# Moving the layer norm's scaling of the 16-row attentions from VectorE to ScalarE

## The chip, the cores and the metric

One core of one Trainium2 chip runs the whole program as a single launch. The metric is device time in microseconds (us). The kernel before took 4759.7 us (median of 3 runs, 4759.58 to 4760.19).

Engine names in the rows: PE is TensorE (PEld its weight loads), DVE is VectorE, ACT is ScalarE, POOL is GpSimd, SPq is SyncE's DMA queue.

## What is computed

The reference is a residual stack of four layers on x of shape 8 x 512 x 256, each an attention and a feed-forward part behind a layer norm. The part that matters here is its first three steps, which share one form: norm, 16 heads of width 16, softmax over 512 keys, output projection, residual.

```python
def _layernorm(x, axis=-1, eps=1e-05):
    m = jnp.mean(x, axis=axis, keepdims=True)
    v = jnp.var(x, axis=axis, keepdims=True)
    return (x - m) / jnp.sqrt(v + eps)
...
x = x + _L0_xattn_ref(_layernorm(x, axis=-1), ctx_1024, ctx_1024, ...)
x = x + _L0_ffn_ref(_layernorm(x, axis=-1), ...)
x = x + _L1_xattn_ref(_layernorm(x, axis=-1), ctx_1024, ...)
```

The second of the three is an attention of x on itself, whose output is scaled by gates (the "mixture").

## The kernel before

The function `softmax_attentions` runs these three steps as 24 **items**: 3 layers x 8 sequences of 512 rows. Items 0 to 7 and 16 to 23 are of kind "cross" (keys and values from the context), items 8 to 15 of kind "mixture". In the trace they fill the stretch from 0 to about 1800 us.

**Rounds and steps.** Every engine has its own instruction stream, and all of them walk the same loop: one round for each item q, 32 steps n in a round. In each step PE makes two score tiles (L715, into `ps_sc`), two tiles from which the maxima are taken (L726, into `ps_max`) and, at odd steps, eight matmuls of probabilities by values (L737). ACT makes one exponential of 1024 columns per step (L642, `probs`). DVE takes two row maxima per step (L461, `maxes`), twelve steps ahead of the exponentials. Both `ps_max` and `ps_sc` are double-buffered.

**The one bank that is shared.** Everything else (transposes, projections, the norm of a later item) goes through a single PSUM bank, `ps_t`. The table `TURNS` says at which step PE fills it with what, and which engine empties it; PE's stream waits until the previous content is taken. The entries of the steps that matter are, for a cross item, 11 and 12 "hT" (the previous item's heads, copied out by ACT, L672), 13 "negmax" (negated maxima of a group of heads, PE L789, copied out by ACT in 1.86 us, L655), 14 "xnT" (the transposed norm of the item two rounds ahead, PE L744, ACT L672), 15 "raw". For a mixture item it is 4 "raw", 5 "negmax", 7 and 8 "xnT".

**The norm.** It is made for the item two rounds ahead (`ahead`). `NORM_AT` sets its start: step 6 where that item is a cross one, step 0 where it is a mixture. From the start on: two steps of `bn_stats` on DVE, then `moments` on DVE (`mv`, L433), then `rstd_of` on POOL (`vareps` L337, `rstd` L340). Four steps after the start and five steps after it, DVE runs `normalised`, two tiles of 128 x 256 each time (L439, `xn`), at the end of the step. When all four tiles of `xn` are done, POOL's `bias` adds the output bias to the item's rows of x (L347, cross items alone), and PE may transpose `xn`.

**Negated maxima.** `negated` (DVE L468 and L470) closes a group of heads; in a cross round group 2 is closed at step 11, between the two calls of `normalised`.

**Splits.** POOL's `split` (L356 to L363) makes the bf16 parts of queries and keys in four operations of about 2 us.

Of the kernel before, what the change touches and what calls it, by code (L numbers as in the profile page):

```python
# [16 lines left out]
F32 = mybir.dt.float32  # L17
BF16 = mybir.dt.bfloat16
U32 = mybir.dt.uint32
ALU = mybir.AluOpType  # L20
ACT = mybir.ActivationFunctionType
AX = mybir.AxisListType

P = 128
# [3 lines left out]
TILES = S // P  # L28
# [102 lines left out]
NORM_AT = {"cross": 6, "mixture": 0}  # L131
# [13 lines left out]
def softmax_attentions(nc, T, G, name, kind):  # L145
# [13 lines left out]
    with Phase(nc, name) as ph:  # L159
# [9 lines left out]
        mv = ph.sb("mv", [P, TILES, 2], F32)  # L169
        vareps = ph.sb("vareps", [P, TILES], F32)  # L170
        rstd = ph.sb("rstd", [P, TILES], F32)
        xn = ph.sb("xn", [P, TILES, D], F32)
        xnT = ph.sb("xnT", [P, C, S], F32)
        qf = ph.sb("qf", [P, C, S], F32)
# [53 lines left out]
        score_ps, probs_ready, probs_used, out_taken = (ph.sem("score_ps"), ph.sem("probs_ready"),  # L228
                                                        ph.sem("probs_used"), ph.sem("out_taken"))
        rden_ready = ph.sem("rden_ready")  # L230
        sp_step, sq_ready, qlen_ready = ph.sem("sp_step"), ph.sem("sq_ready"), ph.sem("qlen_ready")
        rnorm_ready, qtok_ready = ph.sem("rnorm_ready"), ph.sem("qtok_ready")
        gate_step, gexp_ready, ffo_added = ph.sem("gate_step"), ph.sem("gexp_ready"), ph.sem("ffo_added")
# [97 lines left out]
        def _(pool):  # L331
            ones = G["one"][:].unsqueeze(2).broadcast_to([P, C, S])

            def rstd_of(q):

                pool.wait_ge(stats_ready, q.count(TILES, TILES))
                nc.gpsimd.tensor_tensor(vareps[:], mv[:, :, 1], G["eps"][:].broadcast_to([P, TILES]),  # L337
                                        ALU.add).then_inc(vareps_ready, 1)
                pool.wait_ge(vareps_ready, q.count(1, 1))
                nc.gpsimd.tensor_tensor(rstd[:], vareps[:], G["neghalf"][:].broadcast_to([P, TILES]),  # L340
                                        ALU.pow).then_inc(rstd_ready, 1)

            def bias(q):

# [37 lines left out]
            def steps(q):  # L382
# [3 lines left out]
                for n in range(STEPS):  # L386
# [17 lines left out]
                    if ahead.later and after_q in (1, 2):  # L404
                        here, there = (taken["q"], ahead.count(2, 2)) if ahead.cross else (taken["qT"], ahead.own(2, 2))
                        split(ahead, here, there, qf, qparts, q_step, q_split, after_q - 1)

            rstd_of(Item(0))
            nc.gpsimd.memset(vpad[0][:], 1.0).then_inc(vpad_ones, 1)
            nc.gpsimd.memset(vpad[1][:], 1.0).then_inc(vpad_ones, 1)  # L410
# [5 lines left out]
        def _(dve):  # L416
# [18 lines left out]
            def normalised(q, tiles):  # L435
                if tiles[0] == 0:
                    dve.wait_ge(rstd_ready, q.count(1, 1))
                for t in tiles:
                    V.tensor_scalar(xn[:, t, :], q.rows(x_sb, t, 1).rearrange("p a d -> p (a d)"),  # L439
                                    mv[:, t, 0:1], rstd[:, t:t + 1], ALU.subtract, ALU.mult).then_inc(xn_ready, 1)  # L440
# [133 lines left out]
            def steps(q):  # L574
# [3 lines left out]
                for n in range(STEPS):  # L578
# [36 lines left out]
                    if ahead.later:  # L615
                        start = NORM_AT[ahead.kind]
                        if n in (start, start + 1):
                            statistics(ahead, (0, 1) if n == start else (2, 3))
                        if n == start + 2:
                            moments(ahead)  # L620
                        if n in (start + 4, start + 5):
                            normalised(ahead, (0, 1) if n == start + 4 else (2, 3))

            rounds(steps)
            dve.wait_ge(taken["y"], 2 * ITEMS)
# [2 lines left out]
        def _(act):  # L628
# [30 lines left out]
            def take(q, w, c):  # L659
# [12 lines left out]
                    i = nc.scalar.copy({"xnT": xnT, "hT": hT}[w][:, c, :], ps_t[:])  # L672
                i.then_inc(taken[w], 1)

            def steps(q):
                prev = q.plus(-1)
                ahead = q.plus(2)
                if ahead.there and ahead.later and ahead.seq == 0:
                    weights_here(act, ahead)
                for n in range(STEPS):  # L680
                    for mine, w, c in due(q, n):
                        if w == "negmax":
                            take_negmax(mine, c)
                        if w == "q" and not mine.cross and c == 0 and mine.seq == 0:
                            softplus_of_temperature()
                        if w in ("k", "qT", "xnT", "hT") or (w == "q" and mine.cross):
                            take(mine, w, c)
# [2035 lines left out]
```

## Time and profile before

| | |
|---|---|
| median of 3 runs | 4759.7 us |
| the profiled execution | 4758.25 us, its span 4756.4 us |
| 16-row attentions, steady part | 100 to 1700 us of the span |
| PE busy in that part | 1530 of 1600 us |
| DVE / ACT / POOL busy in that part | 1188 / 1022 / 548 us |
| a round of cross items (start to start) | 70.4 us |
| a round of mixture items | 74 to 75 us |

The page gives the busy time of every engine over the span; the table cuts out the part that the change touches. After it come 3000 us of other layers, on which the change has no hand.

### The profile page before, as it was taken

Reading aid. Unit: us, or ns where it says so; the run is one execution under the profiler, and the core shown is the slowest. Engines: PE = TensorE matmul, PEld = TensorE weight load, DVE = VectorE, ACT = ScalarE, POOL = GpSimd, SP = SyncE. Lnnn points to the kernel's source line nnn. Section 1 sums busy time; section 2 is a strip of 40 time slices with the busy share of each in tenths; the row PEclk is TensorE's granted clock in tenths of the full one; section 3 lists DMA queues with packets and bytes.
Section 4 is the critical chain, followed back from the end, with each engine's and each line's share of the span. In section 5 each row is a group of like instructions: output and inputs, shape, how many; then the busy total and the mean of one; then the engine's idle time right before and its main releaser. Section 6 shows DMA issues by size and latency. Waiting matters only on the chain. (4 is left out here: it accounts for less than half of the span.)

```text
span 4756.4 us, 67654 instructions
## 1 busy us (share of the span) xinstructions
PE 4330.5 (91%) x23938; PEld 2408.4 (51%) x23938; DVE 3124.3 (66%) x7497; ACT 2460.3 (52%) x5534; POOL 899.1 (19%) x583
## 2 busy tenths in 40 slices
PE   5999999999999995677576999999999998999998
PEld 2333334443333333455354666666666666555555
DVE  5777777777777775778665667767666766334333
ACT  3666666666666665511232677677767676111111
POOL 2322443533223203511243000000000000000000
PEclk8999999999999997889687999999999999999999
DMA  6445345343444420010200011101101101000001
GB/s 146 76 71 82 65 58 89 54 67 67 67 79 73 72 41 22 1 36 13 90 0 16 27 32 31 30 30 30 35 26 30 35 26 41 33 0 0 0 0 36
DMA packets 182204, 205.16 MB, mean 43 GB/s; under 512 B 43704, under 2 KB 164408, under 8 KB 180256
## 3 DMA queue, kind: packets, MB, share of 16 engines
q1 hardware_dynamic: 181920, 201.45, 21.4%
q8 instruction: 168, 2.75, 0.3%
q14 instruction: 116, 0.95, 0.1%
HBM read 140.64 MB, written 60.78 MB: 42 GB/s over the span
## 5 line engine op out<-in xcount | busy, mean ns | idle before, releaser
L461 DVE TENSOR_REDUCE L0x_maxes<-L0x_ps_max 128x1 f32<-128x512 f32 x1536 | 986.1, 684 | 275.7 <-PE L0x_ps_max L726 271.9
L642 ACT ACTIVATE L0x_probs<-L0x_ps_sc 128x1024 f32<-128x1024 f32 x768 | 778.5, 1026 | 413.6 <-PE L0x_ps_sc L715 407.9
L726 PE MATMUL L0x_ps_max<-L0x_kstack,L0x_qstack 96*128 96x512 bf16 x1536 | 593.9, 387 | 20.6 <-DVE L0x_maxes L461 12.4
L2431 ACT ACTIVATE L3x_pexp<-L3x_ps,L3x_nmax 128x77 f32<-128x77 f32 (+2 forms) x1536 | 600.3, 432 | 0.0
L715 PE MATMUL L0x_ps_sc<-L0x_qstack,L0x_kstack 104*128 104x512 bf16 x1536 | 523.3, 382 | 8.9 <-ACT L0x_probs L642 5.9
L2313 DVE TENSOR_REDUCE L3x_nmax<-L3x_ps 128x2 f32<-128x154 f32 (+2 forms) x768 | 346.2, 506 | 240.3 <-PE L3x_ps L2544 237.9
L737 PE MATMUL L0x_ps_out<-L0x_probs,L0x_vpad 128*32 128x512 f32 x3072 | 411.7, 608 | 9.1 <-ACT L0x_heads_raw L650 8.6
L2439 ACT COPY L3x_pT<-L3x_ps 128x512 f32<-128x512 f32 x512 | 275.0, 593 | 226.6 <-PE L3x_ps L2552 226.2
L1952 ACT ACTIVATE L3f_act_g<-L3f_ps_gu 128x512 f32<-128x512 f32 x128 | 76.4, 597 | 565.2 <-PE L3f_ps_gu L1997 565.2
L726 PEld LDWEIGHTS L0x_ps_max<-L0x_kstack,L0x_qstack 96*128 96x128 bf16 x1536 | 149.0, 97 | 424.8 <-DVE L0x_maxes L461 320.8
L2329 DVE TENSOR_SCALAR L3x_pexp<-L3x_pexp,L3x_rsum 128x77 f32<-128x77 f32 (+2 forms) x1536 | 357.7, 306 | 6.8
L2431 ACT ACTIVATION_READ_ACCUMULATOR L3x_pexp<-L3x_ps,L3x_nmax 128x1 f32 x1536 | 360.3, 235 | 0.0
L1896 DVE TENSOR_TENSOR L3f_h<-L3f_act_g,L3f_ps_gu 128x512 f32<-128x512 f32 x128 | 88.0, 687 | 386.8 <-ACT L3f_act_g L1952 385.6
L2570 PE MATMUL L3x_ps<-L3x_pT,L3x_v 128*64 128x128 f32 x4096 | 279.9, 279 | 0.7 <-ACT L3x_oT L2447 0.7
L2552 PEld LDWEIGHTS L3x_ps<-ident,L3x_pexp 128*128 128x128 f32 x2048 | 239.2, 141 | 73.4 <-issue 55.5
L2274 POOL TENSOR_TENSOR L3x_v<-L3x_v,L3x_relv 128x256 f32<-128x256 f32 x32 | 23.4, 730 | 1290.5 <-ACT L3x_v L2414 1290.5
L2552 PE MATMUL L3x_ps<-ident,L3x_pexp 128*128 128x128 f32 x2048 | 266.1, 273 | 0.9 <-DVE L3x_pexp L2329 0.9
L1997 PE MATMUL L3f_ps_gu<-L3f_xnT,L3f_wg 128*128 128x512 f32 x512 | 243.6, 598 | 9.3 <-DVE x_res L1906 7.1
L2008 PE MATMUL L3f_ps_y<-L3f_wd,L3f_h 128*128 128x256 f32 x1024 | 242.6, 380 | 2.2 <-DVE x_res L1906 2.2
L1997 PE MATMUL L3f_ps_gu<-L3f_xnT,L3f_wu 128*128 128x512 f32 x512 | 240.6, 592 | 0.0
L2570 PEld LDWEIGHTS L3x_ps<-L3x_pT,L3x_v 128*64 128x64 f32 x4096 | 218.3, 136 | 43.4 <-issue 42.4
L2008 PEld LDWEIGHTS L3f_ps_y<-L3f_wd,L3f_h 128*128 128x128 f32 x1024 | 193.3, 190 | 82.0 <-issue 53.8
(356 smaller groups left out, 6993.7 us busy)
## 6 DMA issues: line engine op xcount, KB each, us to landing
L0x_kstack<-parts_scratch SPq DMA_DIRECT2D x144, 256.0 KB, 8.9
L0x_qstack<-parts_scratch SPq DMA_DIRECT2D x144, 256.0 KB, 13.6
parts_scratch<-L0x_kparts SPq DMA_DIRECT2D x24, 768.0 KB, 3.6
parts_scratch<-L0x_qparts SPq DMA_DIRECT2D x24, 768.0 KB, 4.1
rel_scratch<-L3x_rel_e SPq DMA_DIRECT2D x32, 408.0 KB, 2.4
L3x_rel_d<-prob_scratch SPq DMA_DIRECT2D x32, 408.0 KB, 3.1
L0x_kv_in<-in_ctxT SPq DMA_DIRECT2D x16, 512.0 KB, 5.2
L3x_rel_t<-rel_scratch SPq DMA_DIRECT2D x32, 154.0 KB, 2.4
```

Source lines behind the costliest of these rows:

```text
L461: V.tensor_reduce(maxes[:, t, head:head + 1], ps_max[:, unit % 2, :], AX.X, ALU.max).then_inc(max_taken, 1)
L642: nc.scalar.activation(probs[:, n % 4], ps_sc[:, 2 * (n % 2):2 * (n % 2) + 2, :], ACT.Exp, scale=HD ** -0.5).then_inc(probs_ready, 1)
L715: i = nc.tensor.matmul(ps_sc[:, 2 * (n % 2) + j, :], kstack[q.parity][:, head, kt * P:(kt + 1) * P], qstack[q.parity][:, head, :], start=T ...
L726: nc.tensor.matmul(ps_max[:, unit % 2, :], qstack[q.parity][0:ROWS, head, t * P:(t + 1) * P], kstack[q.parity][0:ROWS, head, :], start=Tru ...
L737: i = nc.tensor.matmul(ps_out[32 * j:32 * j + 32, :], vpad[q.parity][:, kt, 4 * g + j, :], probs[:, (pairs + j // 2) % 4, j % 2, :], start ...
L1997: i = nc.tensor.matmul(ps_gu[:, n % 2, k], w[:, ci, n * P:(n + 1) * P], xnT[:, ci, :], start=(ci == 0), stop=(ci == C - 1))
L2008: i = nc.tensor.matmul(ps_y[:, n % 2, 0:D], h[:, e % 2, hc, t * P:(t + 1) * P], wd[:, 2 * e + hc, :], start=(hc == 0), stop=(hc == 1))
L2313: i = V.tensor_reduce(nmax[:, n % 4, s], ps[:, bank:bank + 2, a:b], AX.X, ALU.max, negate=True)
L2329: i = V.tensor_scalar(pexp[:, m % 4, e, a:b], pexp[:, m % 4, e, a:b], rsum[:, m % 4, s, e:e + 1], None, ALU.mult)
L2431: i = nc.scalar.activation(pexp[:, n % 4, e, a:b], ps[:, SB + 2 * (n % 2) + e, a:b], ACT.Exp, bias=nmax[:, n % 4, s, e:e + 1], accum_out=s ...
L2552: i = nc.tensor.transpose(ps[:, TB + e, kt * P:(kt + 1) * P], pexp[:, m % 4, e, kt * P:(kt + 1) * P], ident[:])
L2570: i = nc.tensor.matmul(ps[DIMH * e:DIMH * (e + 1), OB, at:at + P], v[g % 2][:, vt, h * DIMH:(h + 1) * DIMH], pT[:, m % 2, e, kt * P:(kt + ...
```

## The change

The scaling `xn = (x - mean) * rstd` was one VectorE operation per tile. It becomes one ScalarE operation per tile, `xn = x * rstd + mean_shift` with `mean_shift = -mean * rstd`. POOL makes the shift with two more small operations, `negmean` and `mean_shift`, both 128 x 4. Item 0 keeps its scaling on DVE. On ACT the calls stand at the *start* of steps 10 and 11 (cross) or 4 and 5 (mixture), ahead of what ACT does for these steps; on DVE they stood at the *end* of the same steps.

```diff
@@ POOL, rstd_of
-                pool.wait_ge(vareps_ready, q.count(1, 1))
+                nc.gpsimd.tensor_tensor(negmean[:], mv[:, :, 0], negone[:].broadcast_to([P, TILES]),
+                                        ALU.mult).then_inc(vareps_ready, 1)
+                pool.wait_ge(vareps_ready, q.count(2, 2))
+                if q.later:
+                    pool.wait_ge(xn_ready, q.count(TILES, 0))
                 nc.gpsimd.tensor_tensor(rstd[:], vareps[:], G["neghalf"][:].broadcast_to([P, TILES]),
-                                        ALU.pow).then_inc(rstd_ready, 1)
+                                        ALU.pow).then_inc(deviation_ready, 1)
+                pool.wait_ge(deviation_ready, q.count(1, 1))
+                nc.gpsimd.tensor_tensor(mean_shift[:], negmean[:], rstd[:], ALU.mult).then_inc(rstd_ready, 1)
@@ POOL, at the start
+            nc.gpsimd.memset(negone[:], -1.0).then_inc(negone_set, 1)
+            pool.wait_ge(negone_set, 1)
@@ DVE, steps
-                        if n in (start + 4, start + 5):
-                            normalised(ahead, (0, 1) if n == start + 4 else (2, 3))
@@ ACT
+            def normalised(q, tiles):
+                if tiles[0] == 0:
+                    act.wait_ge(rstd_ready, q.count(1, 1))
+                    act.wait_ge(in_bank["xnT"], q.count(2, 0))
+                for t in tiles:
+                    nc.scalar.activation(xn[:, t, :], q.rows(x_sb, t, 1).rearrange("p a d -> p (a d)"), ACT.Identity,
+                                         bias=mean_shift[:, t:t + 1], scale=rstd[:, t:t + 1]).then_inc(xn_ready, 1)
@@ ACT, steps, first thing in a step
+                    if ahead.there and ahead.later:
+                        start = NORM_AT[ahead.kind]
+                        if n in (start + 4, start + 5):
+                            normalised(ahead, (0, 1) if n == start + 4 else (2, 3))
```

In the changed file line numbers are higher: the exponential is L652, the copies of hT and xnT L682, the copy of the heads L660, the negmax copy L665, the new scaling L691; on DVE the maxima are L473, the negated maxima L480 and L482.

ACT, steps 9 to 14 of a cross round (`heads_raw` is the copy of finished head outputs). Before:

```order
L642 ACTIVATE L0x_probs<-L0x_ps_sc 128x1024 x6
L650 COPY L0x_heads_raw<-L0x_ps_out 128x512
L672 COPY L0x_hT<-L0x_ps_t 128x512
L642 ACTIVATE L0x_probs<-L0x_ps_sc 128x1024
L672 COPY L0x_hT<-L0x_ps_t 128x512
L642 ACTIVATE L0x_probs<-L0x_ps_sc 128x1024
L655 CAST L0x_qstack<-L0x_ps_t 8x2048
L642 ACTIVATE L0x_probs<-L0x_ps_sc 128x1024
L672 COPY L0x_xnT<-L0x_ps_t 128x512
```

The same place after:

```order
L652 ACTIVATE L0x_probs<-L0x_ps_sc 128x1024 x5
L691 ACTIVATE L0x_xn<-x_res,L0x_mean_shift,L0x_rstd 128x256 x2
L652 ACTIVATE L0x_probs<-L0x_ps_sc 128x1024
L660 COPY L0x_heads_raw<-L0x_ps_out 128x512
L691 ACTIVATE L0x_xn<-x_res,L0x_mean_shift,L0x_rstd 128x256 x2
L682 COPY L0x_hT<-L0x_ps_t 128x512
L652 ACTIVATE L0x_probs<-L0x_ps_sc 128x1024
L682 COPY L0x_hT<-L0x_ps_t 128x512
L652 ACTIVATE L0x_probs<-L0x_ps_sc 128x1024
L665 CAST L0x_qstack<-L0x_ps_t 8x2048
L652 ACTIVATE L0x_probs<-L0x_ps_sc 128x1024
L682 COPY L0x_xnT<-L0x_ps_t 128x512
```

Two scalings stand ahead of step 10's exponential, two ahead of the first copy of hT.

ACT, steps 3 to 8 of a mixture round, before:

```order
L642 ACTIVATE L0x_probs<-L0x_ps_sc 128x1024 x2
L655 CAST L0x_qstack<-L0x_ps_t 8x2048
L642 ACTIVATE L0x_probs<-L0x_ps_sc 128x1024 x2
L672 COPY L0x_xnT<-L0x_ps_t 128x512
L642 ACTIVATE L0x_probs<-L0x_ps_sc 128x1024
L672 COPY L0x_xnT<-L0x_ps_t 128x512
```

and after:

```order
L652 ACTIVATE L0x_probs<-L0x_ps_sc 128x1024
L691 ACTIVATE L0x_xn<-x_res,L0x_mean_shift,L0x_rstd 128x256 x2
L652 ACTIVATE L0x_probs<-L0x_ps_sc 128x1024
L691 ACTIVATE L0x_xn<-x_res,L0x_mean_shift,L0x_rstd 128x256 x2
L665 CAST L0x_qstack<-L0x_ps_t 8x2048
L652 ACTIVATE L0x_probs<-L0x_ps_sc 128x1024 x2
L682 COPY L0x_xnT<-L0x_ps_t 128x512
```

The second pair stands between step 4's exponential and the negmax copy.

DVE, steps 10 and 11 of a cross round, before:

```order
L461 TENSOR_REDUCE L0x_maxes<-L0x_ps_max 128x1 x2
L439 TENSOR_SCALAR L0x_xn<-x_res,L0x_mv,L0x_rstd 128x256 x2
L461 TENSOR_REDUCE L0x_maxes<-L0x_ps_max 128x1 x2
L468 TENSOR_SCALAR L0x_negmax<-L0x_maxes 128x16
L470 SCALAR_TENSOR_TENSOR L0x_negmax<-L0x_maxes,L0x_negmax 128x16
L439 TENSOR_SCALAR L0x_xn<-x_res,L0x_mv,L0x_rstd 128x256 x2
```

and after:

```order
L473 TENSOR_REDUCE L0x_maxes<-L0x_ps_max 128x1 x4
L480 TENSOR_SCALAR L0x_negmax<-L0x_maxes 128x16
L482 SCALAR_TENSOR_TENSOR L0x_negmax<-L0x_maxes,L0x_negmax 128x16
L473 TENSOR_REDUCE L0x_maxes<-L0x_ps_max 128x1 x6
```

Both pairs are gone from DVE, and the last `xn` no longer stands behind the negated maxima.

## Rows read from the trace of the kernel before

**Rows 1.** Busy time by engine, 100 to 1700 us (start:end, length, engines, PEclk, DMA, GB/s).

```profile
100.00:1700.00 1600.00, 1530.45 (x8012) 610.78 (x8014) 1187.58 (x2336) 1022.37 (x1072) 548.13 (x274) 1.00 0.45 72
```

**Rows 2.** Groups: count, busy, mean ns, idle before; last row: ns least/median/most.

```profile
L439 DVE TENSOR_SCALAR L0x_xn<-x_res,L0x_mv,L0x_rstd 128x256 f32<-128x256 f32 x88 | 32.0, 406 | 0.0
...
L1160 ACT ACTIVATE L1f_xn<-x_res,L1f_shift,L1f_rstd 128x256 f32<-128x256 f32 x32 | 16.5, 589 | 13.3 <-POOL L1f_shift L1051 13.3
...
L1051 POOL TENSOR_TENSOR L1f_shift<-L1f_negmean,L1f_rstd x8: 201/1144/1147, 1816.6 to 1988.6; 128x4 f32<-128x4 f32 x8
```

**Rows 3.** Waits, 100 to 1700 us: who for whom, us in total, times, longest.

```profile
ACT L0x_probs L642 <- PE L0x_ps_sc L715: 376.0, 272, 4.2
PEld L0x_ps_max L726 <- DVE L0x_maxes L461: 283.6, 531, 1.2
...
PEld L0x_ps_t L744 <- ACT L0x_qstack L655: 14.6, 14, 1.3
```

**Rows 4.** ACT in time, steps 10 to 13 of a cross round (start, us, ..., [idle before]).

```profile
1422.12 1.02 ACT L642 ACTIVATE L0x_probs<-L0x_ps_sc 128x1024 f32<-128x1024 f32 x1 [2.77 <-PE L0x_ps_sc L715]
...
1423.50 0.61 ACT L672 COPY L0x_hT<-L0x_ps_t 128x512 f32<-128x512 f32 x1
...
1423.98 1.06 ACT L642 ACTIVATE L0x_probs<-L0x_ps_sc 128x1024 f32<-128x1024 f32 x1
...
1425.42 0.58 ACT L672 COPY L0x_hT<-L0x_ps_t 128x512 f32<-128x512 f32 x1 [0.38 <-PE L0x_ps_t L744]
...
1427.12 1.86 ACT L655 CAST L0x_qstack<-L0x_ps_t 8x2048 bf16<-8x2048 f32 x1
```

**Rows 5.** PE's weight loads in time, fills of `ps_t` in the same steps.

```profile
1424.73 0.42 PEld L744 LDWEIGHTS L0x_ps_t<-ident,L0x_htok 128*128 128x128 f32 x4 [0.84 <-ACT L0x_hT L672]
...
1426.18 0.20 PEld L789 LDWEIGHTS L0x_ps_t<-identb,L0x_negmax 128*8 128x8 bf16 x4 [0.42 <-ACT L0x_hT L672]
...
1429.03 0.42 PEld L744 LDWEIGHTS L0x_ps_t<-ident,L0x_xn 128*128 128x128 f32 x4 [1.04 <-ACT L0x_qstack L655]
```

**Rows 6.** POOL and DVE in time, the same steps.

```profile
1417.65 1.02 POOL L340 TENSOR_TENSOR L0x_rstd<-L0x_vareps,neghalf 128x4 f32<-128x4 f32 x1
...
1423.92 1.28 DVE L461 TENSOR_REDUCE L0x_maxes<-L0x_ps_max 128x1 f32<-128x512 f32 x2
...
1425.23 0.18 DVE L468 TENSOR_SCALAR L0x_negmax<-L0x_maxes 128x16 bf16<-128x16 f32 x1
...
1426.35 2.36 POOL L347 TENSOR_TENSOR x_res<-x_res,L0x_bo_cross 128x1024 f32<-128x1024 f32 x1 [7.68 <-DVE L0x_xn L439]
```

**Rows 7.** POOL, DVE and PE in time, step 27 of the same round.

```profile
1463.13 2.12 POOL L358 TENSOR_TENSOR L0x_qf<-L0x_qf,L0x_qparts 128x1024 f32<-128x1024 f32 x1
1463.19 2.10 DVE L468 TENSOR_SCALAR L0x_negmax<-L0x_maxes 128x16 bf16<-128x16 f32 x1
...
1465.65 0.38 PE L789 MATMUL L0x_ps_t<-identb,L0x_negmax 128*8 128x128 bf16 x4 [1.01 <-DVE L0x_negmax L470]
```

**Rows 8.** POOL, ACT and PE in time, steps 2 to 7 of a mixture round.

```profile
816.34 1.02 POOL L340 TENSOR_TENSOR L0x_rstd<-L0x_vareps,neghalf 128x4 f32<-128x4 f32 x1
...
819.68 1.02 ACT L642 ACTIVATE L0x_probs<-L0x_ps_sc 128x1024 f32<-128x1024 f32 x1 [1.43 <-PE L0x_ps_sc L715]
...
820.73 1.86 ACT L655 CAST L0x_qstack<-L0x_ps_t 8x2048 bf16<-8x2048 f32 x1
...
822.61 1.94 ACT L642 ACTIVATE L0x_probs<-L0x_ps_sc 128x1024 f32<-128x1024 f32 x2
...
823.57 0.63 PE L744 MATMUL L0x_ps_t<-ident,L0x_xn 128*128 128x128 f32 x4 [0.22 <-DVE L0x_xn L439]
...
824.04 0.38 PE L715 MATMUL L0x_ps_sc<-L0x_qstack,L0x_kstack 104*128 104x512 bf16 x1
```

**Rows 9.** POOL and ACT in time, the round that prepares item 16.

```profile
1125.06 1.02 POOL L340 TENSOR_TENSOR L0x_rstd<-L0x_vareps,neghalf 128x4 f32<-128x4 f32 x1
...
1126.57 1.02 ACT L642 ACTIVATE L0x_probs<-L0x_ps_sc 128x1024 f32<-128x1024 f32 x1 [1.11 <-PE L0x_ps_sc L715]
```

More of the change, by code:

```diff
@@ L171, in softmax_attentions @@
         rstd = ph.sb("rstd", [P, TILES], F32)
+        negone = ph.sb("negone", [P, 1], F32)
+        negmean = ph.sb("negmean", [P, TILES], F32)
+        mean_shift = ph.sb("mean_shift", [P, TILES], F32)
         xn = ph.sb("xn", [P, TILES, D], F32)
@@ L230, in softmax_attentions @@
         rden_ready = ph.sem("rden_ready")
+        negone_set, deviation_ready = ph.sem("negone_set"), ph.sem("deviation_ready")
         sp_step, sq_ready, qlen_ready = ph.sem("sp_step"), ph.sem("sq_ready"), ph.sem("qlen_ready")
```

## The prediction, made before the changed kernel ran

> **What bounds the kernel now.** I read four views, from coarse to fine. First the busy time by stretch [rows 1]: in the attentions' steady part PE is busy 1530 of 1600 us, DVE 1188, ACT 1022. PE sets the pace, and both DVE and ACT have room. Then the list of waits [rows 3]: ACT waits 376 us for scores, so most of what ACT is given costs nothing; PE's weight loads stand 284 us waiting for DVE's maxima, which looks as if DVE were worth relieving, but these are short stands (531, at most 1.2 us) next to matmuls that still run, and PE itself is idle only 70 us in the stretch. The third row there is the important one: 14 times, once for each cross item but two, PE stands about a microsecond because ACT has not yet emptied the shared bank of the negmax copy. So at that place, and nearly there alone, ACT and not DVE ends last. The timelines then say where it lies: steps 10 to 14 of a cross round [rows 4, 5, 6], the steps in which the change puts its work. Averages say "ACT has room"; the place says it has none.
>
> **What is removed.** Four DVE operations for each of 23 items, 406 ns each; 88 of them are 32.0 us of DVE's busy time, so a pair is 0.73 us [rows 2]. Gain on the path: at the first pair (before the reduces at 1423.92 [rows 6]) PE is in its values matmuls and goes on with hT at 1424.73, which waits for ACT, not for DVE [rows 5]. At the second pair, DVE's maxima come about 0.35 us earlier, but the next thing PE wants after them is the bank, at 1429.03, and that is released by ACT's negmax copy (1427.12 + 1.86 = 1428.98) [rows 4, 5]. DVE's gain is cut off there: I take 0. In a mixture round PE waited 0.22 us for xn [rows 8]; that wait goes, and its place is taken by ACT's negmax copy, see below. Upper bound of the gain: 14 x 0.35 + 8 x 0.22 = 6.7 us.
>
> **What is added on ACT.** The same operation runs in a later layer of this program: 589 ns for 128 x 256 with a scale and a bias per row [rows 2]. They come there four in a row, eight times, and 16.5 us busy for 32 is 2.06 us for four: each further one takes (2.06 - 0.59) / 3 = 0.49 us of a full queue, a pair 0.98 us.
>
> The Trainium skill speaks against such a move (ScalarE: Activation LUTs, "Rules for kernel authors": for add and multiply use VectorE, not ScalarE). The trace agrees per operation, 589 against 406 ns. Taken as a sum over 23 x 4 operations that difference would be 92 x 0.183 = 17 us; my sum does not use it, since the two engines have different slack.
>
> *Cross round, first pair.* It can start when POOL is done. POOL: rstd starts at 1417.65 now and takes 1.02 [rows 6]; negmean puts about 0.15 in front of it, mean_shift 0.20 behind it [rows 2], with 0.06 us for each wait: about 1419.1, or 1420.0 if mean_shift takes the 1.14 us that it mostly takes in the later layer [rows 2]. ACT sits idle 2.77 us up to 1422.12 [rows 4] and needs 1.1. Hidden by that wait, cost 0 either way.
>
> *Cross round, second pair.* ACT starts it where the copy of hT stood, at 1423.50 [rows 4]. There is no idle time: the copy goes to 1424.48 and ends at 1425.09, where PE wanted the bank at 1424.73. PE goes on at 1425.13: +0.40 us. The exponential behind the copy moves to 1424.96, the second copy to 1425.88 (from 1425.42), the exponential of step 12 to 1426.49, the negmax copy to 1427.54 (from 1427.12), and PE's next fill from 1429.03 to 1429.46: +0.42. From there on everything moves together. Cost 0.42 us.
>
> *A new overlap.* POOL's bias operation (2.36 us) starts 0.08 us behind the last xn. It stood behind the negated maxima [rows 6]. Now the last xn ends at 1423.99 + 0.59 = 1424.58, so the bias starts at 1424.66; and DVE, some 0.6 us earlier without its first pair (1425.23 now [rows 6]; the rest of the 0.73 goes into waiting for the next maximum's matmul), runs L468 at about 1424.65 and L470 at 1424.86. Step 27 shows what then happens [rows 7]: L468, usually 0.18 us, starts 0.06 us behind a POOL operation of 2.12 us and takes 2.10 us, and PE waits 1.01 us for it.
>
> The Trainium skill has this as a lock (SBUF — State Buffer, "Who interferes with whom": whichever of a GpSimd operation and a two-port VectorE operation starts first keeps the shared ports for its whole instruction). The trace agrees at step 27 with 2.10 against 0.18 us. By that rule L468 or L470 is held to the end of the bias, whichever comes first.
>
> So L470 ends at about 1427.1 instead of 1425.6. Step 27 gives PE's rhythm behind it: the fill 0.15 us after L470, eight values matmuls 1.42 us after the fill, the next fill 1.0 us later, 1429.66: +0.62 against before, in place of +0.42 (ACT's negmax copy has some room by then). I take 0.6.
>
> *Mixture round.* First pair: ACT idles from 818.25 (1.43 us before 819.68), and POOL, whose rstd ends at 817.36 now, is ready at 817.8, or 818.7 with the slow mean_shift [rows 2, 8]: hidden, or at worst 0.1 us late. Second pair: between the exponential (819.68) and the negmax copy, which goes from 820.73 to 821.71 and ends at 823.57; the exponential of step 5 moves from 822.61 to 823.59 and ends at 824.61. PE's fill with xnT needs the bank at 823.6, as before (the 0.22 us are lost again); but the score matmul of step 7 at 824.04 [rows 8] needs the bank that this exponential empties: 824.66, +0.62 us.
>
> *Special items.* Items 8 and 16 are prepared in rounds without the value projections that give ACT its long idle time: in item 16's round POOL ends rstd at 1126.1 and, with the added operations, the shift at 1126.5; the first pair then pushes the exponential at 1126.57 [rows 9] by 0.93, and the second pair follows without a gap. About 1.4 us at PE there and 1.1 in item 8's round: 2.5 together, 4.4 at most with the slow mean_shift. Item 2's round has no copies of hT; only the overlap with the bias costs, 0.6 us. Items 0 and 1 are the start: the two POOL operations delay item 0's xn by 0.4 us; item 1's pair runs on an idle ACT.
>
> **The sum.** 12 cross rounds (items 3 to 7, 17 to 23) x 0.6 = 7.2; 7 mixture rounds (items 9 to 15) x 0.62 = 4.3; items 8 and 16 2.5; item 2 0.6; start 0.4. Together +15.0 us. The profiled execution lies 1.45 us below the median (4758.25 against 4759.7), and its 4758.25 us would become 4773.3; against the median: 4774.7 us, +0.32%. A measurement can tell about 0.2% (9.5 us) from no change.
>
> **Rivals.**
>
> A. *No overlap.* If the bias starts after L470 (0.2 us later than I have it; the tie is close), 13 rounds fall back: 12 x 0.42 + 4.3 + 2.5 + 0.4 = 12.2 us, 4771.9. Same sign, part of my forecast's range.
>
> B. *ACT's delay is taken up.* PE stands behind several engines; if the 0.4 to 0.6 us per round come back in a later wait on something that did not move (a DMA, a POOL chain), the loss is half or less: 4760 to 4767. For it: PE is 4% idle [rows 1]. Against it: in the waits nothing but ACT and DVE stands before PE in the steady part, and both start from PE's own results, so they move with it.
>
> C. *DVE was the one to relieve (not slower).* PE's 284 us of stands for maxima [rows 3] shrink, and ACT's pairs fit into its 376 us: 4759.7 - 6.7 = 4753, and down to 4726 if all 23 x 1.46 us of DVE time count. It decides from the point where the copy of hT at step 11 is not on PE's path. Against it: PE's loads at 1424.73, 1426.18 and 1429.03 all end on ACT [rows 5].
>
> D. *The overlap costs its full length.* If DVE's lock delays PE by the whole 2.1 us and not by the difference, 13 x 2.1 + 7.2 = 34 us: 4794. Against it: step 27, where 1.9 us of extra time cost PE a wait of 1.01 [rows 7]. Half of it, 4780 to 4784, is conceivable.
>
> **How the numbers follow.** My forecast with A: 0.70 (4769 to 4779). B 0.15, C 0.05, D 0.10. The range takes the forecast and the near parts of B and D: 4765 to 4783. Faster by over 0.2% only by the far part of C: 0.03. Within 0.2% (up to 4769.2): B, C's near part and the low edge of the forecast: 0.20. Slower 0.77.
>
> **What would show it.** In the changed profile: the new scaling at about 589 ns x 92, no idle time before the second pair; a wait of PE's load of hT's second transposition for ACT of some 0.4 us more per cross round; the period of a cross round 70.8 to 71.1 instead of 70.4 us; L480 or L482 with about 2 us at step 11, with the bias above it in time; PE's score load waiting for `probs` once per mixture round. If cross rounds stay at 70.4 us, the reading of steps 11 to 14 is wrong; if L482 stays at 0.18 us at step 11, rival A holds; if mixture rounds lengthen by more than 1 us, ACT has less room there than I read.

## The result

| | median | runs |
|---|---|---|
| before | 4758.9 us (4753.0 to 4760.2) | 6 |
| after | 4779.6 us (4776.1 to 4784.5) | 6 |
| after, once more | 4777.5 us (4775.2 to 4786.6), beside 4758.6 before | 5 and 18 |

Ratio 1.0047 (95%: 1.0034 to 1.0060); the second time 1.0046 (1.0033 to 1.0060). The change costs about 20 us. 4774.7 us was forecast, in a range of 4765 to 4783: sign and range hold, and the middle is 3 to 5 us short. The profiled executions differ by more: span 4779.1 against 4756.4 us, +22.7.

### The profile after

A small table first: the period of a round, measured in each trace from one item's second fill with `xn` (L744 before, L767 after) to the next item's.

| round of item | before | after | difference | predicted |
|---|---|---|---|---|
| 3, 5 to 7, 20 to 23 (cross) | 70.36 | 70.91 | +0.55 | +0.6 |
| 4 (cross) | 70.36 | 71.27 | +0.92 | +0.6 |
| 12 to 15 (mixture) | 74.13 | 74.77 | +0.64 | +0.62 |
| 9 to 11 (mixture), together | 229.67 | 231.07 | +1.40 | +1.86 |
| 8 | 46.21 | 47.31 | +1.10 | +1.1 |
| 16 | 94.42 | 95.82 | +1.40 | +1.4 |
| 17, 19 | 75.18, 76.11 | 75.72, 76.66 | +0.54, +0.55 | +0.6 |
| 18 | 75.17 | 77.41 | +2.24 | +0.6 |
| second fill of item 2 | 124.20 | 131.09 | +6.89 | +1.0 |

The rows that answer to [rows 2] and [rows 6], from the groups of instructions of after (count, busy, mean ns; idle before):

```profile
L691 ACT ACTIVATE L0x_xn<-x_res,L0x_mean_shift,L0x_rstd 128x256 f32<-128x256 f32 x92 | 49.9, 593 | 9.7 <-POOL L0x_mean_shift L351 9.7
...
L482 DVE SCALAR_TENSOR_TENSOR L0x_negmax<-L0x_maxes,L0x_negmax 128x16 bf16<-128x16 f32 x96 | 50.5, 526 | 3.3
```

and the same second operation in the kernel before:

```profile
L470 DVE SCALAR_TENSOR_TENSOR L0x_negmax<-L0x_maxes,L0x_negmax 128x16 bf16<-128x16 f32 x96 | 23.9, 249 | 3.3
```

The scaling takes 593 ns on ACT, as in the later layer (589). L482 was not touched by the change and costs 26.6 us more: 13 times 2.05 us, once in each round that has the bias and a group to close (four more of its 96 take about 1.8 to 2.0 us in both kernels).

The steps that answer to [rows 4 to 6], in the timeline of after (start, us, instruction, [idle before]). Step 10's exponential starts at 1441.92 here and at 1422.12 in [rows 4]; take off 19.80 to compare.

```profile
1438.70 0.20 POOL L351 TENSOR_TENSOR L0x_mean_shift<-L0x_negmean,L0x_rstd 128x4 f32<-128x4 f32 x1
1439.05 1.08 ACT L691 ACTIVATE L0x_xn<-x_res,L0x_mean_shift,L0x_rstd 128x256 f32<-128x256 f32 x2
...
1441.92 1.02 ACT L652 ACTIVATE L0x_probs<-L0x_ps_sc 128x1024 f32<-128x1024 f32 x1 [1.79 <-PE L0x_ps_sc L738]
...
1443.30 1.10 ACT L691 ACTIVATE L0x_xn<-x_res,L0x_mean_shift,L0x_rstd 128x256 f32<-128x256 f32 x2
...
1444.30 0.58 ACT L682 COPY L0x_hT<-L0x_ps_t 128x512 f32<-128x512 f32 x1
1444.47 0.18 DVE L480 TENSOR_SCALAR L0x_negmax<-L0x_maxes 128x16 bf16<-128x16 f32 x1
1444.48 2.38 POOL L357 TENSOR_TENSOR x_res<-x_res,L0x_bo_cross 128x1024 f32<-128x1024 f32 x1 [5.58 <-ACT L0x_xn L691]
1444.68 2.22 DVE L482 SCALAR_TENSOR_TENSOR L0x_negmax<-L0x_maxes,L0x_negmax 128x16 bf16<-128x16 f32 x1
...
1444.92 0.42 PEld L767 LDWEIGHTS L0x_ps_t<-ident,L0x_htok 128*128 128x128 f32 x4 [1.24 <-ACT L0x_hT L682]
...
1447.04 0.38 PE L812 MATMUL L0x_ps_t<-identb,L0x_negmax 128*8 128x128 bf16 x4 [0.59 <-DVE L0x_negmax L482]
...
1447.46 1.86 ACT L665 CAST L0x_qstack<-L0x_ps_t 8x2048 bf16<-8x2048 f32 x1 [0.17 <-PE L0x_ps_t L812]
...
1449.46 0.42 PEld L767 LDWEIGHTS L0x_ps_t<-ident,L0x_xn 128*128 128x128 f32 x4 [0.84 <-ACT L0x_qstack L665]
```

Read from the top: the first pair (two scalings, 1.08 us) is over 1.79 us before the exponential, so it costs nothing. The second pair leaves no gap, and the copy of hT stands behind it. PE's second load of hT waits 1.24 us for ACT (0.84 in [rows 5]) and comes at 1444.92, that is 1425.12 on the old scale: +0.39. Then the bias starts 0.01 us behind L480, and L482 is held until the bias is over (1444.68 + 2.22 = 1446.90; 1444.48 + 2.38 = 1446.86). PE's fill with the negated maxima now waits for DVE, which it did not do in [rows 5], and comes 1.03 us later than before; the fill with xn comes at 1449.46, 1429.66 on the old scale: +0.63.

The mixture round, timeline of after, steps 4 to 7 (it answers to [rows 8]):

```profile
906.95 1.02 ACT L652 ACTIVATE L0x_probs<-L0x_ps_sc 128x1024 f32<-128x1024 f32 x1 [0.45 <-PE L0x_ps_sc L738]
...
907.87 1.08 ACT L691 ACTIVATE L0x_xn<-x_res,L0x_mean_shift,L0x_rstd 128x256 f32<-128x256 f32 x2
...
908.98 1.86 ACT L665 CAST L0x_qstack<-L0x_ps_t 8x2048 bf16<-8x2048 f32 x1
...
910.86 1.94 ACT L652 ACTIVATE L0x_probs<-L0x_ps_sc 128x1024 f32<-128x1024 f32 x2
...
911.93 0.10 PEld L738 LDWEIGHTS L0x_ps_sc<-L0x_qstack,L0x_kstack 104*128 104x128 bf16 x1 [0.63 <-ACT L0x_probs L652]
```

The last row is the score load that in [rows 8] waited for nothing: now it waits for the exponential that the second pair pushed back.

### The profile page after: what moved, and what is told of

It reads as the page before. It is cut to its first block and busy times, and to the rows that moved or that the text cites. A ratio compares the mean times of both kernels' runs of the same rounds, so it can differ in the third digit from the quotient of the medians.

```text
span 4779.1 us, 67726 instructions
## 1 busy us (share of the span) xinstructions
PE 4333.5 (91%) x23914; PEld 2410.9 (50%) x23938; DVE 3123.3 (65%) x7405; ACT 2504.4 (52%) x5626; POOL 907.5 (19%) x632
## 5 line engine op out<-in xcount | busy, mean ns | idle before, releaser
L473 DVE TENSOR_REDUCE L0x_maxes<-L0x_ps_max 128x1 f32<-128x512 f32 x1536 | 986.5, 685 | 295.7 <-PE L0x_ps_max L749 292.7
L652 ACT ACTIVATE L0x_probs<-L0x_ps_sc 128x1024 f32<-128x1024 f32 x768 | 778.1, 1025 | 388.0 <-PE L0x_ps_sc L738 383.1
```

Of the source, the lines that this page charges most:

```text
L473: V.tensor_reduce(maxes[:, t, head:head + 1], ps_max[:, unit % 2, :], AX.X, ALU.max).then_inc(max_taken, 1)
L652: nc.scalar.activation(probs[:, n % 4], ps_sc[:, 2 * (n % 2):2 * (n % 2) + 2, :], ACT.Exp, scale=HD ** -0.5).then_inc(probs_ready, 1)
```

## The experiments

All ratios are to the kernel before, measured on the same chip. The trace's rounds tell more than the totals: most of these kernels lie a few us apart, and the intervals of the ratios reach 4 to 7 us to either side.

### Both kernels again

The first is the changed kernel without an edit, the second the kernel before.

> The changed kernel once more, unchanged. What is open is its start: in the first profile item 2's transposed norm came 6.8 us later than in the kernel before, where I had 1.0. Theory S (the start's delay belongs to the change, by a TensorE stretch at the lower clock and slower loads behind it): again 6 to 7 us at item 2, total 16 to 22 us above the kernel before. Rival N (it is chance, drawn anew by every execution): item 2's shift comes out elsewhere between 1 and 7 us. In both, cross rounds last 70.9 us and mixture rounds 74.7, exactly as in the first profile.

> The kernel before once more, for a second profile of its start. Theory S: item 2's transposed norm at 117.3 us as in the first profile, within 1 us, and the first low stretch of TensorE's clock in the same place. Rival N: it comes some us later or earlier.

4777.5 us (ratio above) and 4758.9 us (1.0005, 0.9996 to 1.0014). The rounds of the table repeat to 0.03 us, but for those in which TensorE's clock was low (items 9 to 11, 17 and 18, of which more below): item 17's takes 77.33 us in the second profile of after, against 75.72. The start does not repeat either: item 2's second fill comes 3.15 us later in the second profile of before than in the first, and 0.57 us earlier in that of after. For the kernel before this is what rival N said, and theory S, which wanted it within 1 us, missed; for after theory S held, with 6.3 us against before's first profile.

### All four tiles of a cross item ahead of step 10's exponential

```diff
-                        if n in (start + 4, start + 5):
+                        if ahead.cross:
+                            if n == start + 4:
+                                normalised(ahead, (0, 1, 2, 3))
+                        elif n in (start + 4, start + 5):
```

> In rounds that prepare a cross item all four scalings stand at the start of step 10 on ScalarE, in its 2.8 us of idle time, none at step 11; mixture rounds as in the changed kernel. My theory (the loss is the place, the second pair stands ahead of the copy of hT that TensorE waits for): cross rounds return to 70.4 us from 70.9, 13 rounds x 0.55 = 7 us less than the changed kernel. VectorE's negated maxima at step 11 take 0.18 us again, since the bias starts about 2.9 us earlier and is over in time. Rival (ScalarE has simply too much work in a cross round): 70.9 us stays, total as the changed kernel.

4771.9 us, 1.0028 (1.0018 to 1.0039). Cross rounds are at 70.37 us, as before the change, mixture rounds at 74.77. In ACT's and POOL's timeline of the same round:

```profile
1434.28 2.06 ACT L691 ACTIVATE L0x_xn<-x_res,L0x_mean_shift,L0x_rstd 128x256 f32<-128x256 f32 x4
1436.42 2.36 POOL L357 TENSOR_TENSOR x_res<-x_res,L0x_bo_cross 128x1024 f32<-128x1024 f32 x1 [2.29 <-ACT L0x_xn L691]
...
1437.15 1.02 ACT L652 ACTIVATE L0x_probs<-L0x_ps_sc 128x1024 f32<-128x1024 f32 x1 [0.81 <-PE L0x_ps_sc L741]
...
1439.91 0.18 DVE L482 SCALAR_TENSOR_TENSOR L0x_negmax<-L0x_maxes,L0x_negmax 128x16 bf16<-128x16 f32 x1
```

The same 2.06 us of ACT's work fit into its idle time with 0.81 us to spare, and the bias is over before L482. So the cross rounds' whole +0.55 us comes from the place of the second pair (and with it of the bias), none of it from ACT's longer operation as such. Item 16's round shows the other side: four scalings ahead of the exponential, where there is little idle time, make it 97.78 instead of 95.82 us. TensorE waits 1.98 us for ACT there, and just behind this wait its clock is low; about 1.7 us of the round are this low stretch, of which more below.

```profile
1140.01 1.42 PE L763 MATMUL L0x_ps_out<-L0x_probs,L0x_vpad 128*32 128x512 f32 x8 [1.98 <-ACT L0x_heads_raw L660]
```

### The bias held until the negated maxima are done

```diff
+                        if q.there:
+                            pool.wait_ge(negmax_ready, q.count(4, 3))
```

> The changed kernel with GpSimd's bias held back until the negated maxima of step 11 are done (one more wait on GpSimd). My theory: VectorE's second negating operation returns from 2.22 to 0.18 us, and of the 0.55 us per cross round 0.42 remain, which is ScalarE's part: 70.8 us a round, total 1 to 2 us below the changed kernel. Rival (the overlap is the whole loss): 70.4 us a round. Rival (it costs nothing beside ScalarE's delay): 70.9 us.

4774.8 us, 1.0037 (1.0023 to 1.0051). Cross rounds 70.78: +0.42 against before, which is rival A's figure. The overlap is worth 0.13 us per round, not 2. In DVE's and POOL's timeline:

```profile
1439.58 0.18 DVE L484 SCALAR_TENSOR_TENSOR L0x_negmax<-L0x_maxes,L0x_negmax 128x16 bf16<-128x16 f32 x1
1439.84 2.35 POOL L357 TENSOR_TENSOR x_res<-x_res,L0x_bo_cross 128x1024 f32<-128x1024 f32 x1 [6.04 <-DVE L0x_negmax L484]
```

The operation of 2.22 us is back at 0.18, with the bias behind it. The other 0.42 are ACT's.

### The scaling on VectorE, of one column only

The kernel before, with 255 of 256 columns of the scaling left out from item 1 on, so that DVE is relieved in part and ACT gets nothing: an operation of one column still takes 265 ns in place of 406, two in a row 0.45 us in place of 0.73.

```diff
-                    V.tensor_scalar(xn[:, t, :], q.rows(x_sb, t, 1).rearrange("p a d -> p (a d)"),
+                    w = 1 if q.later else D
+                    V.tensor_scalar(xn[:, t, 0:w], q.rows(x_sb, t, 1).rearrange("p a d -> p (a d)")[:, 0:w],
```

> The kernel before, with VectorE's scaling cut to one column of 256 from item 1 on; the other 255 columns keep item 0's values, so this part of the norm is left out. It measures what VectorE's scaling costs by itself. My theory: VectorE is not what the round waits for, cross rounds 70.4 us or at most 0.1 shorter, mixture rounds at most 0.2 us shorter, total 0 to 3 us below the kernel before. Rival (VectorE bounds): 0.3 us a cross round and more, 7 us and up to 30 in all.

4754.1 us, 0.9992 (0.9983 to 1.0001). Cross rounds 70.38: no gain from DVE there. The run above says the same with all four scalings gone from DVE (70.37), and so it settles rival C for the cross rounds. Mixture rounds take 73.80 instead of 74.13 us, a gain of 0.33: 8 x 0.33 = 2.6 us in all. What the rest of DVE's time would give in a mixture round wasn't measured with ACT left alone.

### The start apart

In one kernel only items 0 and 1 are as before, in the other only they are changed.

```diff
-                    if ahead.there and ahead.later:
+                    if ahead.there and ahead.later and (ahead.number > 1):
```

```diff
-                    if ahead.there and ahead.later:
+                    if ahead.there and ahead.later and (ahead.number == 1):
```

(VectorE has the scaling of the items that ScalarE doesn't. In the first kernel POOL leaves out the two operations for item 0 alone, and item 1 still gets its shift; in the second it makes them for items 0 and 1 alone.)

> Items 0 and 1 prepared as in the kernel before (VectorE scales, no shift for item 0), all later items as in the changed kernel. Theory S (the start's 6 us belong to the change): item 2's transposed norm at most 1 us later than in the kernel before, total 15 to 16 us above it. Rival N (chance): item 2 comes anywhere, as in other profiles, total not told apart from the changed kernel's.

> Items 0 and 1 prepared as in the changed kernel, all later items as in the kernel before. Theory S: item 2's transposed norm 5 to 7 us later than in the kernel before and the rounds behind it at 70.4 and 74.1 us, total 5 to 7 us above the kernel before. Rival N: the shift at item 2 differs from that, 0.4 to 7 us.

4775.7 us, 1.0043 (1.0029 to 1.0057), and 4760.3 us, 1.0009 (1.0000 to 1.0018). Both point to a cost of the start of 2 to 4 us, and neither proves it. Item 2's second fill comes 3.6 us after that of before's first profile in the one and 7.9 us in the other; theory S had at most 1 us and 5 to 7, and missed in both. What happens is seen when the timelines of the first 60 us are laid side by side. Before:

```profile
8.77 4.57 DVE L439 TENSOR_SCALAR L0x_xn<-x_res,L0x_mv,L0x_rstd 128x256 f32<-128x256 f32 x4 [1.41 <-POOL L0x_rstd L340]
...
18.38 3.78 PE L749 MATMUL L0x_ps_t<-L0x_kv_in,L0x_wk_cross 128*128 128x512 f32 x4 [0.68 <-ACT L0x_xnT L672]
...
22.94 1.98 PE L749 MATMUL L0x_ps_t<-L0x_kv_in,L0x_wk_cross 128*128 128x512 f32 x4 [0.78 <-ACT L0x_kf L664]
...
56.71 3.48 PE L749 MATMUL L0x_ps_t<-L0x_kv_in,L0x_wk_cross 128*128 128x512 f32 x4 [10.38 <-DMA L0x_kv_in<-in_ctxT]
```

After:

```profile
9.16 4.55 DVE L451 TENSOR_SCALAR L0x_xn<-x_res,L0x_mv,L0x_rstd 128x256 f32<-128x256 f32 x4 [1.90 <-POOL L0x_mean_shift L351]
...
18.76 3.78 PE L772 MATMUL L0x_ps_t<-L0x_kv_in,L0x_wk_cross 128*128 128x512 f32 x4 [0.68 <-ACT L0x_xnT L682]
...
23.31 3.78 PE L772 MATMUL L0x_ps_t<-L0x_kv_in,L0x_wk_cross 128*128 128x512 f32 x4 [0.78 <-ACT L0x_kf L674]
...
27.87 3.76 PE L772 MATMUL L0x_ps_t<-L0x_xnT,L0x_wq_cross 128*128 128x512 f32 x4 [0.78 <-ACT L0x_kf L674]
...
62.29 3.60 PE L772 MATMUL L0x_ps_t<-L0x_kv_in,L0x_wk_cross 128*128 128x512 f32 x4 [14.49 <-DMA L0x_kv_in<-in_ctxT]
```

The two POOL operations put the first xn 0.39 us later (9.16 against 8.77), as predicted. But in before the second projection already runs at twice the rate of the first (1.98 against 3.78 us for the same four matmuls), while in after two more of them run at 3.8 us, which is 3.6 us later by there. The loads of item 1's context then come later too. The granted clock shows where the rate changes, if it is read with care: its first record in the trace starts at 22.24 us in before, at full rate, and at 31.47 us in after, and there the single matmuls go from 1061 to 592 ns. Ahead of its first record a slice prints 1.00 though nothing is recorded. The row at 56.71 us in before, 3.48 us for the four matmuls, lies for the most part in a stretch that was granted half the clock:

```profile
36.00:59.00 23.00, 8.28 (x19) 5.13 (x20) 11.05 (x29) 9.55 (x18) 3.81 (x3) 0.50 1.10 163
```

How often PE speeds up early is not set by the change alone: over the seven profiles whose items 0 and 1 are about as before (with those of the later experiments; one has item 1 scaled in one column, and some have item 1's shift made on POOL), item 2's second fill comes -0.5, 0, 1.4, 1.7, 3.1, 3.6 and 3.7 us after before's first profile; over the seven with a changed start 2.1, 2.8, 4.2, 4.9, 6.3, 6.9 and 7.9. The means are 1.9 and 5.0. The groups overlap, so 3 us is an estimate, with item 2's own overlap in four of the second group and once in the first. The clock's first record accounts for a part: it starts at 21.5 to 22.7 us in five of the first group and two of the second, at 27.4 to 27.8 in one and three, at 31.5 in one and two. Among profiles of one such time the second group is still 1.3, 1.4 and 4.3 us later in the mean. Fourteen profiles can't tell whether the change makes a late speed-up more likely. The first profile of before, the one that the prediction had, was an early one.

### Cross items alone, early

The kernel before, with the cross items from 2 on scaled by ScalarE, all four tiles at step 10. (GpSimd makes the shift for every item from 1 on.)

```diff
-                        if n in (start + 4, start + 5):
+                        if not (ahead.cross and ahead.number > 1) and n in (start + 4, start + 5):
                             normalised(ahead, (0, 1) if n == start + 4 else (2, 3))
@@ ACT
+                    if ahead.there and ahead.later and (ahead.cross and ahead.number > 1):
+                        start = NORM_AT[ahead.kind]
+                        if n == start + 4:
+                            normalised(ahead, (0, 1, 2, 3))
```

> The best version that my theory has: only cross items from item 16 and items 2 to 7 on ScalarE, all four scalings at step 10; mixture items and items 0 and 1 on VectorE as in the kernel before. My theory: no copy that TensorE waits for is behind a scaling, and VectorE's time was free: cross rounds 70.4, mixture rounds 74.1, total within 2 us of the kernel before. If VectorE's relief is worth something, it shows here as a cross round under 70.4 us. Rival: ScalarE's load itself costs, 0.3 us a cross round and more.

4762.6 us, 1.0014 (1.0005 to 1.0023). Cross rounds 70.37 and mixture rounds 74.12, both as before; item 8's round is at 46.21, since item 8 is a mixture item and left to VectorE. Item 16's round is 97.41 instead of 94.42, of which a low stretch at 1133 us, behind a wait of PE of 1.98 us for ACT as in the kernel with all four tiles early, is about 1.7. So 3.0 of the 6.3 us that this kernel loses are lost in that one round; they are the larger part of why the expectation, within 2 us of the kernel before, missed.

### Items up to 15, and all but 16

Rounds 17 to 19 hold what the sum had not: in after, item 18's round is 1.7 us longer than its kind. The busy times by stretch of after show it (length, busy of PE, PEld, DVE, ACT, POOL, then the granted clock of PE):

```profile
1220.00:1230.00 10.00, 9.08 (x58) 3.43 (x51) 8.57 (x14) 8.88 (x11) 2.38 (x1) 1.00 1.13 145
1230.00:1240.00 10.00, 9.63 (x44) 4.61 (x43) 4.71 (x11) 4.07 (x5) 0.00 (x0) 0.83 0.49 49
1240.00:1250.00 10.00, 9.51 (x49) 3.99 (x47) 7.29 (x23) 6.38 (x7) 4.02 (x2) 1.00 0.01 2
```

A mean of 0.83 over 10 us means that 3.4 of them were granted half the rate, 1.2 in place of 2.4 GHz: 1.7 us of work not done, which is what the round is longer. Three such stretches stand in before, at 560, 640 and 710 us, and after has low ones at 640 to 660 and 720 to 740. The one at 1230 us is new.

What TensorE did ahead of a fall can be read too. The three in before (565.0, 640.1 and 715.1 us in the trace's clock records) come 0.5 to 1.3 us behind a stand of 2.40 us for the negated maxima, the first row below. In the kernels with all four tiles early, the falls at 1133.3 and 1140.6 us come 0.6 to 1.0 us behind the stand of 1.98 us. At the one of 1236.4 us in after there is no such stand; what ends 1.7 us ahead of it are 16 matmuls of 17 columns, which count as busy:

```profile
564.45 0.38 PE L789 MATMUL L0x_ps_t<-identb,L0x_negmax 128*8 128x128 bf16 x4 [2.40 <-DVE L0x_negmax L470]
```

```profile
1232.71 1.96 PE L828 MATMUL L0x_ps_t<-L0x_wgate_mixture,L0x_hT 128*128 128x17 f32 x16
```

The same 16 stand 0.3 to 1.7 us ahead of all ten falls between 1140 and 1310 us that have no stand of 1.98 us ahead of them. But they stand there three times in every kernel, 42 times in the fourteen profiles, and mostly no fall follows.

Two kernels ask whether the new stretch comes with ScalarE's scalings of items 16 to 23, or with item 16's alone.

```diff
-                    if ahead.there and ahead.later:
+                    if ahead.there and ahead.later and (ahead.number < 16):
```

```diff
-                    if ahead.there and ahead.later:
+                    if ahead.there and ahead.later and (ahead.number != 16):
```

> The changed kernel, but for items 16 to 23, which VectorE scales as before (the POOL operations stay as changed). Question: do the low stretches of TensorE's granted clock between 1130 and 1310 us come from the ScalarE scalings of the cross items from 16 on? They stood in all six profiles that had those and in none of the four without. Theory (they come from there): no such stretch after 1100 us, item 16's round at 94.4 us and not 95.8, the rounds of items 17 and 19 to 23 at 70.36 and not 70.91, item 18 in line with them; items 3 to 7 and 9 to 15 as in the changed kernel (70.91 and 74.77). Total: the changed kernel minus 1.4 for item 16, minus 7 x 0.55, minus about 2 for the stretches: about 7 us less, 4772. Rival (the stretches come by chance, or from whatever came earlier in the kernel): one stands between 1130 and 1310 us here too, rounds outside it at 70.36, and the total is 5 us below the changed kernel.

> The changed kernel, but item 16 alone is scaled by VectorE as before. The low stretches of the granted clock between 1130 and 1310 us may be set off by item 16's round, the one in which ScalarE's scalings hold up TensorE most (1.40 us in one round, at 1125 us). Theory (item 16 sets them off): none between 1130 and 1310 us, item 16's round 94.4 us, the rounds of 17 and 19 to 23 still at 70.91, item 18 at the usual +0.55; total 3 to 4 us below the changed kernel. Rival (each cross round with ScalarE's scalings can set one off): a stretch is still there, in item 17's round or later, total 1.4 us below the changed kernel. The step of 1.4 to 4 us lies near what the medians can tell; the trace's rounds decide.

Up to 15: 4771.4 us, 1.0032 (1.0020 to 1.0044). Item 16's round 94.41, the rounds after it 75.19, 75.18, 76.12 and 70.37, all as in before, and no low stretch from 740 to 1800 us. All but 16: 4778.0 us, 1.0045 (1.0031 to 1.0059); item 16's round is 94.41, and two low stretches stand at 1150 and 1230 us (rounds 17 and 18 take 77.3 us each). So item 16's round doesn't set them off, though the expectation had it so.

### Mixture items shared between the engines

The kernel before, but each mixture item from 9 on has its first pair scaled by ScalarE at step 4 and its second by VectorE at the end of step 4. (GpSimd makes the shift for every item from 1 on.)

```diff
+                        if ahead.number < 9 or ahead.cross:
+                            if n in (start + 4, start + 5):
+                                normalised(ahead, (0, 1) if n == start + 4 else (2, 3))
+                        elif n == start + 4:
+                            normalised(ahead, (2, 3))
@@ ACT
+                    if 9 <= ahead.number < 16 and n == NORM_AT["mixture"] + 4:
+                        normalised(ahead, (0, 1))
```

> The kernel before, but for the mixture items 9 to 15: their first two tiles are scaled by ScalarE at step 4, where it stands idle for 1.43 us before the exponential, and their last two by VectorE at the end of step 4 instead of step 5. Items 0 to 8 and 16 to 23 are scaled as in the kernel before. It asks whether VectorE's scalings cost the mixture rounds anything: with 255 of 256 columns left out, these rounds fell from 74.13 to 73.80 us. Theory (the 0.2 to 0.3 us are TensorE's wait for the last xn, and ScalarE's first pair is hidden in its idle time): rounds of items 9 to 15 at 73.8 to 73.9, cross rounds at 70.36; total 2 us less than the kernel before, which the medians can't tell. Rival (ScalarE's first pair comes too late because the shift takes 1.14 us, or pushes step 4's exponential and with it the negmax copy): mixture rounds 74.1 to 74.4, no gain.

> The same kernel as mixture_shared, a second profile. In the first, the granted clock was low once between 1130 and 1310 us (1140 to 1150), in the round of item 17, though the items from 16 on are scaled by VectorE there. Theory 1 (a low stretch there hangs on small shifts of the timing that a kernel has in every execution): it stands there again, item 17's round at 76.8 us. Theory 2 (chance from execution to execution, which ScalarE's scalings from 16 on make more likely): no low stretch after 1100 us, item 17's round at 75.18. In both the rounds of items 12 to 15 are 73.8 us.

4757.6 us beside 4757.1 for before: 1.0001 (0.9992 to 1.0010). The one run of the second profile took 4755.6 beside 4755.2. Mixture rounds are at 73.79, 0.34 us faster, in both profiles, as expected. But item 17's round takes 76.79 and 76.80 us: a low stretch, though no item from 16 on is scaled by ScalarE. The same 10 us in this kernel and, below, in the kernel before:

```profile
1140.00:1150.00 10.00, 9.68 (x36) 4.17 (x36) 4.05 (x12) 4.32 (x7) 0.00 (x0) 0.83 0.00 0
```

```profile
1140.00:1150.00 10.00, 9.68 (x54) 4.76 (x47) 4.17 (x12) 4.20 (x8) 0.00 (x0) 1.00 0.00 0
```

TensorE's, VectorE's and ScalarE's busy times hardly differ; the clock does. Equal busy time isn't equal work: 16 matmuls of 17 columns count as busy in full, and they end at 1140.5 us in the shared kernel and at 1142.5 in before. The gain of 7 x 0.34 = 2.4 us is mostly given back in one round of a layer that was not edited, at the same place in two executions. The theory that such a stretch needs ScalarE's scalings from 16 on falls here.

## Why the prediction came out as it did

**The sum's steady part is right to a tenth of a microsecond per round.** The cross rounds' +0.55 stands against 0.6; the fill with xn lies at +0.63 in its own round and 0.08 come back later in the round (rival B, in small). The mixture rounds' +0.64 stands against 0.62, and items 8 and 16 are as forecast, 1.10 and 1.40. Added up from the table, 12 x 0.55 + 0.37 (item 4's extra) + 7 x 0.64 + 2.5 = 14.0 us, and the prediction had 14.0. (Items 9 to 11 count here as the other mixture items; what their low stretches change comes below.) Item 4's extra stands in the six profiles of kernels that have both item 1 and the items from 2 on scaled by ScalarE, and in no other: VectorE's first residual add (L577) starts 0.35 us later behind its matmuls in that round, after 2.27 us of idle time in place of 1.92, and what it waits for wasn't found. What carried it was to ask at each place which engine releases the shared bank, and not how much idle time ACT has on average.

**The first pair: hidden, as said.** 1.79 us were left. The slow form of mean_shift (1.14 us) did not come: all 24 took 0.20.

**The overlap: predicted, and confirmed with its size.** 13 times L482 is held, and holding the bias back gives 0.13 us per round; A's 0.42 and the forecast's 0.6 differ by 0.18. The Trainium skill's lock (SBUF — State Buffer, "Who interferes with whom": the one that issues first has the shared ports for its whole instruction) gives the same picture: L480 started 0.01 us ahead of the bias and took its usual 0.18, and L482, behind it, took 2.22 beside the bias's 2.38. Rival D, which took the whole length, priced the wrong thing: PE comes for the negated maxima only 1.5 us after DVE has them (1441.29 against 1439.76 us where the bias was held), so most of the 2 us is hidden.

**DVE's gain: nothing, as said.** At least 0.33 us per mixture round were there to be had (the waiting for xn was put at 0.22), and the changed kernel does not have them: PE's fill with xn waits for ACT's negmax copy there.

The Trainium skill's rule for add and multiply (ScalarE: Activation LUTs, "Rules for kernel authors"), taken as the difference of the durations over 92 operations, would have given 17 us, nearer to the total than the sum was. It is near by accident: the same 2.06 us of ScalarE's work, moved one step ahead, cost the cross rounds nothing.

**What was missed.** The term that failed is the start, put at 0.4 us because two POOL operations delay the first xn by 0.4. They do, by 0.39, but PE's first projections stayed at half the rate for longer, and then the item's loads were late: about 3 us by the means of seven profiles each, with a spread of several us from execution to execution, part of which comes without the change. The second miss has no term in the sum at all: PE's granted clock fell once or twice more between 1130 and 1310 us, about 1.7 us each time. Such a stretch stands in all seven profiles that scale cross items from 16 on with ScalarE, and in two of the other seven, both of them of the one kernel with shared mixture items. With 14.0 for the rounds, 3.1 up to item 2 (start and overlap) and 1.7 to 3.4 for the clock, the account is 18.8 to 20.5 us, against 20.7 and 19.0 measured. In the two first profiles it is 6.9 up to item 2, 14.0 for the rounds, 1.7 for item 18's stretch, 0.5 less for the low stretches between 560 and 740 us, and 0.8 behind item 23's fill, where the low stretch at about 1820 us lasts 6.8 us in after and the one at 1804 us 3.4 in before: 22.9 against 22.7. The kernel without ScalarE's scalings from 16 on agrees: 1.4 for item 16, 7 x 0.55 and 1.7 make 7.0 us less; the ratios, 1.0047 and 1.0032, give 7.1, known to some 8 us. The forecast's range held the total because it was wide enough, not because it had a term for the missing 3 to 5 us.

**What stays open.** Which of the places with a stand or with narrow matmuls brings a fall of the clock. It follows small shifts of the timing (a kernel has one at the same place in both profiles: 1236 us in after, 1141 and 1142 in the shared one; after had one more, at 1157, in its second profile only), and neither item 16's round nor ScalarE's scalings are needed for it. The start's 3 us is likely, not shown.

## What to carry to other kernels

An engine with 36% of idle time had none at the place where the work was put, and 2 us of it one step earlier: look for the step at which the engine waits, and for what stands behind the new work in its queue. Moving an operation to another engine also moves everything released by it; here GpSimd's bias came 1.7 us earlier in the round, 1.1 us of it relative to VectorE's chain, and ran into it. And where TensorE is 95% busy, single rounds can gain or lose 1.7 us by its clock, so judge an edit by the periods of undisturbed rounds, and by several profiles where the start matters.

## What the runs showed of the hardware

- A VectorE operation of 0.18 us that starts 0.20 us behind a GpSimd operation of 2.38 us takes 2.22 us, though it works on 128 x 16 elements; it happened 13 times (2.21 to 2.28 us). One that started 0.01 us ahead of the same operation was not touched.
- TensorE's granted clock fell to half for about 3.4 us at a time in the slices shown, with the engine 96 and 97% busy; the slice at 1140 us was as busy in the kernel that kept the full clock. Ahead of the falls stood a wait of 2.40 or 1.98 us, or 16 matmuls of 17 columns that count as busy (1.96 us).
- At the start the same four matmuls took 3.78 us once in before and three times in after, ahead of 1.98 us. The trace's first clock record starts where they speed up (22.24 and 31.47 us); the 1.00 that a slice prints ahead of it stands for no record.
- 128 x 256 on ScalarE with scale and bias per row: 593 ns each, 1.08 us for two in a row, 2.06 for four.
